# First layer of a four-layer model: norms, weight preparation, projections and scan in one program

## The reference, cut to what matters

```python
xn = _layernorm(x)
x = x + attn(xn, ...) + ffn(xn, ...)

# attn: norm again, with gain and shift
xn = (x - mu) * rsqrt(var + 1e-5) * g + b
u, z = split(xn @ W_in)                     # 256 channels each
uc = silu(causal_conv(u, conv_w, 4 taps) + conv_b)
dbc = uc @ W_x                              # 8 + 16 + 16 columns
dt = softplus(dbc[..., :8] @ W_dt + b_dt)
h = h * exp(dt * A) + (dt * uc) * B         # per token, 16 states a channel
y = einsum('bds,bs->bd', h, C) + uc * Dskip
return x + (y * silu(z)) @ W_out

# ffn: fp4_quant_dequant on x, on the three weights and on the hidden values
```

## Time and profile before

| | us |
|---|---|
| median of 3 runs | 750.08 (748.85 to 752.56) |
| profiled execution | 754.06, of which the span from first to last instruction is 752.3 |
| PE, DVE, ACT, POOL busy in the span | 605.3, 508.2, 321.1, 380.6 |

### The profile page before, as it was taken

The page is one execution under the profiler, slowest core; times in us unless marked ns, Lnnn a source line. Parts: engine busy times, 40 slices in busy tenths (PEclk is TensorE's granted clock), DMA queues, the critical chain, the costliest instruction groups (busy, mean ns, idle before and its releaser), DMA issues. The chain is left out here.

```text
span 752.3 us, 8493 instructions
## 1 busy us (share of the span) xinstructions
PE 605.3 (80%) x2794; PEld 367.7 (49%) x2794; DVE 508.2 (68%) x902; ACT 321.1 (43%) x611; POOL 380.6 (51%) x297
## 2 busy tenths in 40 slices
PE   0598838889889888778758867799899999898886
PEld 0233212223223232346545565599688867555555
DVE  7677777999999999488816358764333656354542
ACT  1336645554545544223236995342221236333341
POOL 0025525999999999457643017195911640022220
PEclk9999956999999999989997999899999999999999
DMA  4000007765567555200006001141512100000001
GB/s 110 0 3 4 4 4 152 154 154 127 136 137 129 134 124 93 64 0 1 0 18 175 1 1 15 29 128 43 160 36 56 42 15 1 0 1 1 0 1 56
DMA packets 47541, 43.49 MB, mean 58 GB/s; under 512 B 12375, under 2 KB 32777, under 8 KB 47498
## 3 DMA queue, kind: packets, MB, share of 16 engines
q1 hardware_dynamic: 46474, 40.86, 23.4%
q0 software_dynamic: 1024, 2.10, 0.9%
HBM read 36.85 MB, written 6.09 MB: 57 GB/s over the span
## 5 line engine op out<-in xcount | busy, mean ns | idle before, releaser
L569 PE MATMUL bank<-l0s_hc,all_ident 128*128 128x512 f32 x256 | 127.5, 623 | 25.9 <-POOL l0s_hc L616 25.8
L585 ACT ACTIVATE bank<-l_DT,l_negA 128x512 f32<-128x512 f32 x128 | 88.3, 691 | 95.6 <-DVE l0s_h L643 95.6
L643 DVE TENSOR_TENSOR_SCAN l0s_h<-bank,l0s_carry,l0s_h 128x512 f32<-128x512 f32 x96 | 115.5, 1259 | 0.1
L569 PEld LDWEIGHTS bank<-l0s_hc,all_ident 128*128 128x128 f32 x256 | 44.4, 191 | 107.5 <-issue 53.8
L609 POOL TENSOR_TENSOR l0s_h<-l_DTU,l0s_b_all 128x1024 f32<-128x1024 f32 x32 | 63.9, 1998 | 19.1 <-DMA l0s_c_rest<-bc_rows 19.1
L616 POOL TENSOR_TENSOR l0s_hc<-l0s_h,l0s_c_rest 128x1024 f32<-128x1024 f32 x32 | 63.7, 1996 | 1.7 <-POOL l0s_hc L616 1.7
L616 POOL TENSOR_TENSOR l0s_hc<-l0s_h,all_XF 128x1024 f32<-128x1024 f32 x32 | 63.6, 1997 | 0.1
L559 PE MATMUL bank<-l_DBC,all_ident 40*128 40x512 f32 x64 | 38.0, 681 | 7.9 <-PEq L391 7.9
L415 PE MATMUL bank<-l_XM,l_wins 128*128 128x512 f32 x64 | 34.6, 693 | 7.3 <-ACT l_ZS L467 4.5
L632 DVE TENSOR_TENSOR l0s_h<-l_DTU,bank 128x1024 f32<-128x1024 f32 x32 | 38.2, 1192 | 2.4 <-PE bank L559 2.4
L643 DVE TENSOR_TENSOR_SCAN l0s_h<-bank,l0s_h 128x512 f32<-128x512 f32 x32 | 37.0, 1202 | 3.6 <-POOL l0s_h L609 3.5
(11 more groups left out here) (399 smaller groups left out, 1431.3 us busy)
## 6 DMA issues: line engine op xcount, KB each, us to landing
l0s_b_all<-bc_rows SPq DMA_DIRECT2D x32, 256.0 KB, 3.8
l0s_c_rest<-bc_rows SPq DMA_DIRECT2D x16, 512.0 KB, 6.1
all_XF<-bc_rows SPq DMA_DIRECT2D x16, 512.0 KB, 6.3
l_wall<-in_L_ffn_W SPq DMA_DIRECT2D x14, 256.0 KB, 5.1
all_X<-in_L_attn_x SPq DMA_DIRECT2D x4, 256.0 KB, 3.6
gx<-l1m_TD SPq DMA_DIRECT2D x1, 1024.0 KB, 5.2
gy<-l1m_TD SPq DMA_DIRECT2D x1, 1024.0 KB, 8.6
out<-all_X SPq DMA_DIRECT2D x4, 256.0 KB, 2.3
```

Source lines behind the costliest of these rows:

```text
L569: last = nc.tensor.matmul(bank_y[j][:, :], S.ident[:, :], hc[n % CRING][:, j, :], start=False, stop=(n % DS == DS - 1))
L585: nc.scalar.activation(decay(n, j)[:, :], DT[:, j, block_of(n)], ACT.Exp, scale=negA[:, j, n % DS:n % DS + 1]).then_inc(decay_ready, 1)
L643: nc.vector.tensor_tensor_scan(h[n % RING][:, j, :], decay(n, j)[:, :], h[n % RING][:, j, :], before, ALU.mult, ALU.add).then_inc(h_ready, 1)
```

## The change

The five programs from the first norm to the scan become one (`l0s`), with semaphores in the place of block ends.

- Norms: the second norm's variance is worked out as var/(var+eps) from the first one's moments; ACT makes the second norm from X directly (`norm2`), DVE makes the first one later (`norm`), POOL adds it to X (`keep_norm`).
- SP's loads are put in another order: convolution weights and W_in first, then the columns and projection weights, then those of the feed-forward part.
- Softplus is max(x, 0) plus ln(1 + exp(-|x|)): ACT takes Abs, Exp, Square and Ln, DVE has the maximum, one series step, the minimum and the sum. Its buffers are parts of the scan's rings, of DTU and of OUTF.
- Weights: DVE scales (`fp4_scale`), POOL rounds.
- The last block's softplus is split: Exp and Square ahead of the scan's loop, Ln and the DVE steps inside it, behind steps 2 and 5 (`SERIES_3 = 4`).

Helpers not shown: `second_variance` (reciprocal and two products, then `v2_ready`), `second_gain` (reciprocal and two products, then `gains_ready`), `moments` (as before). The core of the diff:

```diff
+        q_of = [slot(0), slot(1)] + 2 * [S.OUTF[:, 0:W2]...]
+        ln_of = [slot(2), slot(RING + 1)] + 2 * [S.OUTF[:, W2:2 * W2]...]
...
+                    def step_size(b):
+                        pe.wait_ge(dbc_ready, b + 1)
+                        for j in range(JT):
+                            if b:
+                                pe.wait_ge(max_ready, JT * (b - 1) + j + 1)
...
+                    turn(0)
+                    conv(0, 0)
+                    turn(1)
+                    conv(0, 1)
+                    for b in range(NBLK):
+                        gate_in(b)
+                        if b == NBLK - 1:
+                            turn_weight(1)
+                        project(b)
+                        if b + 2 < NBLK:
+                            turn(b + 2)
+                        if b + 1 < NBLK:
+                            conv(b + 1, 0)
+                        if b == NBLK - 1:
+                            turn_weight(2)
+                        step_size(b)
+                        if b + 1 < NBLK:
+                            conv(b + 1, 1)
+                        if b == 1:
+                            turn_weight(0)
...
+                    def magnitude(b):
+                        for j in range(JT):
+                            act.wait_ge(dt_done, JT * b + j + 1)
+                            nc.scalar.activation(DTU[:, j, blk(b)], S.bank[6 + j][:, :], ACT.Abs, bias=b_dt[j]).then_inc(abs_ready, 1)
+                    def exponent(b):
+                        act.wait_ge(abs_ready, JT * (b + 1))
+                        nc.scalar.activation(DTU[:, :, blk(b)], DTU[:, :, blk(b)], ACT.Exp, scale=-1.0).then_inc(ex_ready, 1)
+                    def square(b):
...
+                        nc.scalar.activation(q_of[b], DTU[:, :, blk(b)], ACT.Square, bias=third[:, 0:1], scale=3.0 ** -0.5).then_inc(q_ready, 1)
...
+                    deviations(0)
+                    norm2(0)
+                    deviations(1)
+                    norm2(1)
+                    mixer_in(0)
+                    norm2(2)
+                    mixer_in(1)
+                    norm2(3)
+                    silu_u(0, 0)
+                    silu_u(0, 1)
+                    silu_z(0)
+                    keep_dbc(0)
+                    mixer_in(2)
+                    silu_u(1, 0)
+                    magnitude(0)
+                    silu_u(1, 1)
+                    silu_z(1)
+                    keep_dbc(1)
+                    mixer_in(3)
+                    silu_u(2, 0)
+                    magnitude(1)
+                    exponent(0)
+                    exponent(1)
...
+                    square(0)
+                    square(1)
...
+                    silu_u(2, 1)
+                    silu_z(2)
+                    keep_dbc(2)
+                    logarithm(0)
+                    logarithm(1)
+                    keep_weight(0)
+                    silu_u(3, 0)
+                    magnitude(2)
+                    exponent(2)
+                    square(2)
+                    silu_u(3, 1)
+                    silu_z(3)
+                    keep_weight(1)
+                    keep_dbc(3)
+                    logarithm(2)
+                    keep_weight(2)
+                    magnitude(3)
...
                     for n in range(2):
                         for j in range(JT):
                             forget(n, j)
+                    exponent(3)
+                    square(3)
                     for n in range(STEPS):
...
+                        if n == SERIES_3 - 2:
+                            logarithm(3)
...
+                    for b in range(NBLK):
+                        keep_norm(b)
+                    round_x(0)
...
+                    for b in range(1, NBLK):
+                        round_x(b)
+                    for b in range(NBLK - 1):
+                        scaled_u(b)
 
                     input_of(1)
...
+                    moments(0)
+                    moments(1)
+                    moments(2)
+                    second_variance(0)
+                    moments(3)
+                    second_gain(0)
+                    dve.wait_ge(cw_wide, 1)
+                    dve.wait_ge(win_loaded, 16)
...
+                        if j == 0:
+                            second_variance(1)
+                    second_gain(1)
+                    for b in range(NBLK):
+                        norm(b)
+                    x_part(0)
...
+                    positive(0)
+                    x_part(1)
+                    x_part(2)
+                    positive(1)
+                    x_part(3)
+                    power_series(0)
+                    power_series(1)
+                    softplus(0)
+                    softplus(1)
+                    positive(2)
+                    power_series(2)
+                    softplus(2)
+                    positive(3)
+
                     input_of(0)
...
+                        if n == SERIES_3:
+                            power_series(3)
+                            softplus(3)
+                            dve.wait_ge(dt_ready, NBLK)
+                            nc.vector.tensor_tensor(DTU[:, :, blk(NBLK - 1)], DT[:, :, blk(NBLK - 1)], UC[:, :, blk(NBLK - 1)], ALU.mult).then_inc(dtu_ready, 1)
```

More of the change, by code:

```diff
@@ new lines, in conv @@
+                    def conv(b, j):
+                        pe.wait_ge(xm_ready, b + 1)
+                        pe.wait_ge(wins_ready, j + 1)
+                        if b:
+                            pe.wait_ge(u_ready, JT * (b - 1) + j + 1)
+                        else:
+                            pe.wait_ge(zeroed, 4)
+                        for k in range(DC):
+                            last = nc.tensor.matmul(S.bank[j][:, :], wins[:, k, j * P:(j + 1) * P],
+                                                    XM[:, b * BLK + k:b * BLK + k + BLK], start=(k == 0), stop=(k == DC - 1))
+                        last.then_inc(u_done, 1)
@@ new lines, in norm2, with mixer_in @@
+                    def norm2(b):
+                        act.wait_ge(gains_ready, b // 2 + 1)
+                        for k in range(TPB):
+                            t = b * TPB + k
+                            last = nc.scalar.activation(S.TMPT[:, t, :], S.X[:, t, :], ACT.Identity, bias=shift2[:, t:t + 1], scale=g2[:, t:t + 1])
+                        last.then_inc(normed2, 1)
+                    def mixer_in(b):
+                        act.wait_ge(turned, b + 1)
+                        if b == 0:
+                            act.wait_ge(ln_loaded, 32)
+                        nc.scalar.activation(XM[:, DC - 1 + b * BLK:DC - 1 + (b + 1) * BLK], S.bank[5][:, :], ACT.Identity,
+                                             bias=b_col, scale=g_col).then_inc(xm_ready, 1)
@@ new lines, in silu_u, with silu_z @@
+                    def silu_u(b, j):
+                        act.wait_ge(u_done, JT * b + j + 1)
+                        if b == 0 and j == 0:
+                            act.wait_ge(proj_loaded, 96)
+                        nc.scalar.activation(UC[:, j, blk(b)], S.bank[j][:, :], ACT.Silu, bias=conv_b[j]).then_inc(u_ready, 1)
+                    def silu_z(b):
+                        for j in range(JT):
+                            act.wait_ge(z_done, JT * b + j + 1)
+                            nc.scalar.activation(ZS[:, j, blk(b)], S.bank[2 + j][:, :], ACT.Silu).then_inc(z_ready, 1)
@@ new lines, in positive, with power_series @@
+                    def positive(b):
+                        for j in range(JT):
+                            dve.wait_ge(abs_ready, JT * b + j + 1)
+                            nc.vector.tensor_scalar(DT[:, j, blk(b)], S.bank[6 + j][:, :], b_dt[j], 0.0, ALU.add, ALU.max).then_inc(max_ready, 1)
+                    def power_series(b):
+                        dve.wait_ge(q_ready, b + 1)
+                        nc.vector.scalar_tensor_tensor(q_of[b], q_of[b], 13.0 / 16.0, DTU[:, :, blk(b)], ALU.add, ALU.mult).then_inc(series, 1)
```

551 lines of the change are left out of this document (240 added, 311 removed).

## The result

| | us |
|---|---|
| kernel before, first four runs | 751.32 (748.85 to 753.93) |
| changed kernel, first four runs | 723.33 (720.6 to 729.19) |
| ratio | 0.9637, 95% interval 0.9568 to 0.9707 |
| profiled execution after | 720.6, of which the span is 718.9 |

The change makes the kernel 3.6% faster. silu_u, silu_z, keep_dbc, magnitude (Abs), exponent, square and logarithm are ACT's steps on them. power_series and softplus are DVE's steps, and scaled_u is POOL's product DTU. The stretches of the changed kernel answer to the earlier trace rows.

What follows compares the result with a forecast made beforehand. POOL bound the scan, and no engine was full ahead of it. First input 35.6 us sooner less 4.4 lost in the scan is 31.2: profiled 754.06 becomes 722.9, less 4.0 gives 718.9 us, range 710 to 729.

Steps and rivals of the forecast that it cites:

- First convolution: Ahead of the projections: PE's first convolution starts at 14.7 us instead of 34.66, after weights at 6.5 and gains at 9.6.
- PE's stretch: From the first convolution on, PE is the late engine; block 1's step size, step_size(1), ends at 47.7 us.
- ACT's stretch: After step_size(1), ACT is the late engine until logarithm(2) ends at 79.1 us; project(2) and project(3) cold, 3.4 each.
- rival (a): Projections and scan: project(2) and project(3) at full clock, 1.7 us each; inserted steps 4.9, not 6.8; 713.6 us; chance 0.20.
- my own sign of being wrong: In the changed profile: first convolution late, project(2) and (3) warm, more ACT loads, or other POOL gaps in the scan.
- Abs and Square without a table load: On ACT ahead of the scan: Abs and Square priced like Silu and Exp, 0.69 and 1.06 us, without own load.
- rival (b): On ACT ahead of the scan: Abs and Square change tables, six loads, 7.7 us more; 726.6 us; chance 0.19, drain included.
- First input: Start of the scan: POOL's first scan input comes at 84.1 us instead of 119.69, 35.6 sooner.
- In the scan: Block 3's four added DVE steps make POOL idle 6.4 us; scan idle 7.0 against 2.6 before, 4.4 lost.
- From the profiled run to the median: Whole kernel: 4.0 us taken off 722.9, as the median of three runs, 750.08, lay below the profiled 754.06.
- rival (d): In the scan: PE left at half clock throughout, 32 pairs at 2.7 us more, 87 in all; 806 us; chance 0.02.

Runs made afterwards that it cites:

- the late fetch: Changed kernel with SP storing the B and C rows of all four blocks before fetching the first of them: one execution, 720.96 us.
- the other order: Changed kernel with conv(3,0) ahead of project(2) and silu_u(3,0) ahead of keep_dbc(2): 720.12 us with Square on DVE, 721.79 us (one execution) without.

## Why the prediction was right, and where its steps failed

Forecast 718.9, range 710 to 729, faster: measured 723.33 and, repeated, 723.62. Range and sign held, and the mechanism too: the gain is the first input's, less a loss in the scan. Point by point:

- **First convolution** 14.7: measured 14.57. Weights 6.5 (6.22), gains 9.6 (9.51), both held; the two runs that disturb them (weights late, norm as before) move the scan by 4.5 and 10.2.
- **PE's stretch** to step_size(1) 47.7: measured 46.5. The three turns took 0.60 to 0.66 us each, not 1.0.
- **ACT's stretch** to logarithm(2) 79.1: measured 76.08. Of the 3.0 us, 1.1 came with PE's stretch, 0.5 from project(2) (2.86 for 3.4) and 1.5 from project(3) (1.91 for 3.4). This step failed as a rule: I priced both as cold because PE had idled. Half of rival (a), and half of my own sign of being wrong, came true with project(3). Below is the evidence that the idle time doesn't decide it.
- **Abs and Square without a table load**: held; rival (b) is out. The Trainium skill's 2.66 us for a switch ("ScalarE: Activation LUTs", "What ACT_TABLE_LOAD costs") doesn't hold here: three switches taken away gave 3.9, the waits that they had covered included, and in the rows above the next ACTIVATE starts 1.29 or 1.30 after the load began.
- **First input** 84.1: 80.99, by the same 3.0 us. Forecast gain 35.6, measured 38.7.
- **In the scan** 4.4 lost: 6.85. The gap itself was near, 5.98 for 6.4. Two terms were missing. The read-out beside the stretched steps took 0.98 more; I had priced what POOL does to DVE and not what DVE does to POOL. And I let go of the idle time of the scan before (2.6 us), of which 0.86 and 0.79 at two block borders and 0.58 at the start stayed. Idle and stretch are 0.58 + 5.98 + 1.65 + 0.98 = 9.2 against 2.6, which is 6.6 of the 6.85. The idle time at the two borders is not the change's: it stands in the kernel before (0.85 and 0.86) and without the four steps (0.86 and 0.79) as well.
- The two misses, 3.1 for it and 2.4 against it, nearly cancel: the span's gain was forecast as 31.2 and would have been 31.9, with the 1.5 behind the scan 33.4.
- **From the profiled run to the median**: the step that cost most on the total. The sum gave 722.9 for an execution like the profiled one, which is within 0.7 of both medians. I then took off 4.0, since the median of before was 750.08 in three runs. In 11 runs it is 755.13, in 11 others 754.88, in 7 752.49. The three runs were too few to place it, and the 4.0 was not a property of the profiled run. That 722.9 is so near is in part luck: the two misses cancel, and the profiled execution of the change took 720.6, 2.3 less than the sum and 2.7 less than its own median.
- **Clock in the scan**, rival (d): 0.95 granted against 0.98 before, and the scan unmoved by it, as the four DVE steps account for all of its length; with 0.94 granted in the repeated run it was 195.44 again.

What stays open: why the part behind the scan, the same code in all of them, takes 441.4 to 446.9 us from one profiled execution to another. It is larger than several of the effects measured here (project(2)'s 0.95, the fetch's 1.1), which therefore stand on the first input and not on the total. Behind the scan PE is busy 365.97 us at a granted 0.95 in the shortest and 368.2 at 0.94 in one of the longest; that goes with it and is not shown to be its cause. The first input has a spread of its own too: conv(0,0), the same code in the changed kernel and all of its variants, took 5.10 to 6.74 us in their profiled executions.

## What to carry to other kernels

Follow the latest engine of each stretch and take work from that one alone: Square off ACT gave 2.3 us though it is more work in all, while an order that filled PE's idle time gave nothing once that idle time was gone. When a step is moved beside an engine that is the bound, price both sides, what it costs the step and what it costs the bound engine. A profiled execution that lies 4 us off the median of three runs is no reason to shift a forecast by 4 us; the spread of the runs (748 to 758 for the kernel before) belongs in the range instead. And before an edit is credited with a shift in one execution, what TensorE's clock did in that execution has to be taken off on both sides: it made 2.79 look like 3.74 here, and 8.7 like 10.2.

## What the runs showed of the hardware that I had not expected

**The clock after a pause.** project(2) stands behind 2.73 us of idle PE in nine of the profiled executions, behind the same convolution half and gate_in. It took 2.86, 2.60, 2.33, 1.91, 2.80, 1.91, 1.91, 3.28 and 1.91 us. The first rows are from the kernel with the steps spread, the second from that with the late fetch; each shows conv(0,0), project(2) and conv(3,0) behind it:

```profile
14.45 5.10 PE L291 MATMUL bank<-l_XM,l_wins 128*128 128x512 f32 x8 [2.25 <-ACT l_XM L410]
54.45 3.28 PE L309 MATMUL bank<-l_UC,l_wx 128*40 128x512 f32 x4 [2.73 <-ACT l_UC L417]
57.66 3.98 PE L291 MATMUL bank<-l_XM,l_wins 128*128 128x512 f32 x8
```

```profile
14.81 6.15 PE L291 MATMUL bank<-l_XM,l_wins 128*128 128x512 f32 x8 [2.25 <-ACT l_XM L410]
55.86 1.91 PE L309 MATMUL bank<-l_UC,l_wx 128*40 128x512 f32 x4 [2.73 <-ACT l_UC L417]
57.70 3.70 PE L291 MATMUL bank<-l_XM,l_wins 128*128 128x512 f32 x8
```

1.91 is full clock (2.4 GHz) throughout; the longer ones ran in part at half (1.2 GHz). From 55 to 58 us the clock granted is 0.50 in the first and 1.00 in the second. The rows hold more than a chance of two values.

- In the five executions with a long project(2), it and conv(3,0) behind it take 7.26 or 7.27 us together, against 5.61 in the other four. So the spell at half clock cost PE 1.65 each time; what differs is how much of it falls on project(2), for which ACT waits.
- conv(0,0), some 40 us ahead, took 5.52, 5.78, 6.05, 5.58 and 5.10 us in those five. With the project(2) of the same execution this is 8.38 each time. In the other four it took 6.15 to 6.74. So the level at project(2) goes with how the first convolution ran. Why they are tied is not shown.
- project(3) took 1.91 in all eight executions that had idled 0.65 to 1.75 us ahead of it, 3.48 and 3.59 after 2.01 and 2.02, and 1.91 after 2.02 in the late fetch. But a short pause is no safety: in the two kernels with the other order PE idled 0.68 ahead of step_size(2), and conv(3,1) behind it took 5.27 and 5.40 us instead of 3.70.

The idle time alone does not tell the level, and a forecast has to carry both values in its range.

**Two elementwise engines at once.** DVE's 128x1024 step with two inputs in SBUF took 1.23 us alone. In the scan it took 1.88 to 2.83 in the change and when spread, where the operation of POOL that followed took 2.98 instead of 2.00, and 5.24 meeting two, which took 2.00 each. In the projections one took 3.25 and the scaled_u beside it 3.27 instead of 2.35. Which of the two gives way was not to be seen from who is recorded as starting first.
